# A third bank for the transposed scores of the fourth stage, its value products in the tail's bank, and a new order of all pieces

## What is computed

```python
x = x + _L0_attn_ref(_layernorm(x, axis=-1), L0_attn_w_q, L0_attn_w_k, L0_attn_w_v, L0_attn_w_o)
x = x + _L0_xattn_ref(16, 128, 256, L0_xattn_w, L0_xattn_u, _layernorm(x, axis=-1), ctx_2048)
x = x + _L0_ffn_ref(_layernorm(x, axis=-1), L0_ffn_w1, L0_ffn_w2, L0_ffn_w3)
x = x + _L1_attn_ref(_layernorm(x, axis=-1), L1_attn_Wq, L1_attn_Wk, L1_attn_Wv, L1_attn_Wo)
x = x + _L1_xattn_ref(_layernorm(x, axis=-1), ctx_2048, L1_xattn_Wq, L1_xattn_Wk, L1_xattn_Wv, L1_xattn_Wsk, L1_xattn_Wsv, L1_xattn_Wo)
x = x + _L1_ffn_ref(_layernorm(x, axis=-1), L1_ffn_W_base, L1_ffn_b_base, L1_ffn_A_s, L1_ffn_B_s, L1_ffn_A_r, L1_ffn_B_r, L1_ffn_W_router, L1_ffn_b_router)
```

```python
bias = jnp.concatenate([alibi, alibi], axis=-1)
delta = -rel
ssm_mask = (delta >= 0) & (delta < W_SSM)
att_mask = (delta >= 0) & (delta < W_ATT)
mask = jnp.concatenate([ssm_mask, att_mask], axis=-1)
scores = jnp.einsum('bhqd,bhkd->bhqk', q, k) / np.sqrt(D).astype(np.float32)
scores = scores + bias[None]
scores = jnp.where(mask[None, None], scores, -jnp.inf)
wei = jax.nn.softmax(scores, axis=-1)
return jnp.einsum('bhqk,bhkd->bhqd', wei, v)
```

## Time and profile before

| | us |
|---|---|
| median of 3 runs | 701.42 |
| lowest and highest | 701.37, 702.06 |
| span of the profiled execution | 699.8 |
| PE busy | 592.3 |
| DVE busy | 564.3 |
| ACT busy | 485.4 |
| POOL busy | 357.8 |

### The profile page before, as it was taken

The page is one execution under the profiler, slowest core; times in us unless marked ns, Lnnn a source line. Parts: engine busy times, 40 slices in busy tenths (PEclk is TensorE's granted clock), DMA queues, the critical chain, the costliest instruction groups (busy, mean ns, idle before and its releaser), DMA issues.

```text
span 699.8 us, 20088 instructions
## 1 busy us (share of the span) xinstructions
PE 592.3 (85%) x7268; PEld 351.6 (50%) x7268; DVE 564.3 (81%) x1487; ACT 485.4 (69%) x1197; POOL 357.8 (51%) x600
## 2 busy tenths in 40 slices
PE   0579789776688888999999978899999999989995
PEld 0256556454465667644444434454454445445653
DVE  5699988889989997879999767777777777777885
ACT  3689999887878756568888764577667677665531
POOL 3336766798999989766665312424323323312110
PEclk9999999988999999999999999999999999999998
DMA  7486984211110002545455534534444344320101
GB/s 268 106 171 148 243 118 92 65 58 50 45 39 31 24 1 51 76 77 77 78 78 84 98 54 82 99 74 71 78 86 71 66 89 76 53 49 19 39 32 37
DMA packets 162819, 55.16 MB, mean 79 GB/s; under 512 B 148961, under 2 KB 160545, under 8 KB 162465
## 3 DMA queue, kind: packets, MB, share of 16 engines
q1 hardware_dynamic: 160672, 53.75, 38.2%
q0 software_dynamic: 2048, 0.14, 0.2%
HBM read 16.89 MB, written 5.24 MB: 32 GB/s over the span
## 4 chain that ended last, share of the span: by engine, by line
PE 49%; POOL 14%; DVE 13%; issue 9%; ACT 6%; DMA 6%; SPq 3%; ACTq 0%; DVEq 0%; POOLq 0%
PE bank L1330 5%; DMA l1a_kT<-k_stack 3%; PE bank L1277 3%; PE bank L999 3%; PE bank L1302 3%; PE bank L1263 3%; POOL mix_hidden_parts L1493 2%; PE bank L1356 2%; PE bank L1284 2%; PE bank L987 2%; PE bank L1336 2%; PE bank L1306 2%; PE bank L1019 2%; PE bank L1859 2%; PE bank L960 2%
## 5 line engine op out<-in xcount | busy, mean ns | idle before, releaser
L1178 DVE TENSOR_REDUCE l1x_neg_max<-bank 128x2 f16<-128x448 f32 (+1 forms) x192 | 117.2, 639 | 35.4 <-PE bank L1284 34.1
L1232 ACT ACTIVATE l1x_probs<-bank 128x512 f32<-128x512 f32 x192 | 104.5, 596 | 51.3 <-PE bank L1316 28.9
L1134 POOL DMA_DIRECT2D l1x_qT<-l1x_neg_maxT x64 | 36.2, 577 | 136.4 <-ACT l1x_neg_maxT L1228 136.2
L886 DVE TENSOR_REDUCE l1a_neg_max<-bank 128x4 f16<-128x512 f32 x128 | 83.0, 680 | 15.2 <-PE bank L973 14.2
L933 ACT ACTIVATE l1a_probs<-bank 128x512 f32<-128x512 f32 x128 | 70.1, 598 | 20.4 <-PE bank L987 20.0
L1679 PE MATMUL bank<-mix_xT_parts,w_ternary 128*128 128x256 f16 x384 | 50.8, 284 | 10.1 <-DVE mix_hidden L1561 10.1
L1679 PEld LDWEIGHTS bank<-mix_xT_parts,w_ternary 128*128 128x128 f16 x384 | 37.6, 102 | 19.1 <-DVE mix_hidden L1561 7.9
L568 DVE TENSOR_REDUCE l_neg_max<-bank 128x4 f16<-128x512 f32 x64 | 41.9, 679 | 6.0 <-PE bank L697 5.8
L1493 POOL TENSOR_TENSOR mix_hidden_parts<-mix_hidden,mix_hidden_parts 128x256 f16<-128x256 f32 x48 | 37.8, 792 | 6.5 <-ACT mix_hidden_parts L1624 6.2
L640 ACT ACTIVATE l_probs<-bank 128x512 f32<-128x512 f32 x64 | 35.6, 621 | 1.4 <-PE bank L720 1.0
L1284 PE MATMUL bank<-l1x_kT,l1x_qT 64*64 64x224 f16 (+1 forms) x1024 | 36.2, 236 | 0.0
(11 more groups left out here) (266 smaller groups left out, 1741.4 us busy)
## 6 DMA issues: line engine op xcount, KB each, us to landing
ctx_projected<-mix_ctx_projected SPq DMA_DIRECT2D x16, 192.0 KB, 1.9
l1x_ctx_projected<-ctx_projected SPq DMA_DIRECT2D x16, 160.0 KB, 2.6
x_residual<-x_in SPq DMA_DIRECT2D x4, 512.0 KB, 4.7
mix_ctx_in<-ctx_in SPq DMA_DIRECT2D x16, 128.0 KB, 2.0
out_dram<-moe_out SPq DMA_DIRECT2D x16, 128.0 KB, 1.7
w_f<-w_in SPq DMA_DIRECT2D x2, 704.0 KB, 8.5
w_attn_f<-w_l_in SPq DMA_DIRECT2D x1, 1024.0 KB, 6.5
q_stack<-q_begin_in SPq DMA_DIRECT2D x1, 1024.0 KB, 5.2
```

Source lines behind the costliest of these rows:

```text
L886: dve.tensor_reduce(mm[:, 16 * j + 4 * s:16 * j + 4 * s + 4], b_s[c % 3][:].rearrange("p (r k) -> p r k", k=P), AX.X, ALU.max, negate=True ...
L1178: dve.tensor_reduce(mm[:, first:first + count], scores, AX.X, ALU.max, negate=True).then_inc(s_max, 1)
L1232: act.activation(prob[:, c, :], b_st[c % 2][:], ACT.Exp).then_inc(s_exp, 1)
```

## The change

The work of each instruction stays as it was, and none is added or taken away. Three things change.

**The fourth stage's banks.** ST rotates over banks 5, 6 and 7, so that step c needs one exp less than before; PV sums into bank 0, the tail's, and waits for the addition to x of the batch before (semaphore s_x), where it waited for ACT's copy of the last sum; T1 loses two waits.

**The order of the fourth stage and of all others.** One table PHASES gives each piece one virtual place relative to its batch. Its numbers are new for every stage, so the order differs on every engine.

**Setup and late loads.** Each step of the setup has its own virtual time in a table STEPS.

```diff
-    b_tail, b_proj, b_s, b_st, b_ot = banks[0], banks[1], banks[2:5], banks[5:7], banks[7]
+    b_tail, b_proj, b_s, b_st = banks[0], banks[1], banks[2:5], banks[5:8]
...
-                act.activation(prob[:, c, :], b_st[c % 2][:], ACT.Exp).then_inc(s_exp, 1)
+                act.activation(prob[:, c, :], b_st[c % 3][:], ACT.Exp).then_inc(s_exp, 1)
...
-                act.copy(ots[:, bp, :], b_ot[:]).then_inc(s_oe, 1)
+                act.copy(ots[:, bp, :], b_tail[:]).then_inc(s_oe, 1)
...
-                    take(pe, prev.left, 5, 6)
-                wait(pe, s_exp, 12 * b + 2 * c)
-                tiles = [(b_st[j][64 * u:64 * u + 64, :], slice(64 * j, 64 * j + 64), slice(64 * u, 64 * u + 64))
+                    take(pe, prev.left, 5, 6, 7)
+                wait(pe, s_exp, 12 * b + 2 * c - 1)
+                tiles = [(b_st[(2 * c + j) % 3][64 * u:64 * u + 64, :], slice(64 * j, 64 * j + 64), slice(64 * u, 64 * u + 64))
...
-                    take(pe, prev.left, 7)
+                    take(pe, prev.left, 0)
                 pe.wait_ge(s_exp, b * 12 + 6 * (c + 1))
-                wait(pe, s_oe, b)
+                wait(pe, s_x, b)
...
-                    pe.matmul(b_ot[32 * x:32 * x + 32, :], v_flat[:, b % 3, col:col + 32], prob[:, 6 * c + x, :],
+                    pe.matmul(b_tail[32 * x:32 * x + 32, :], v_flat[:, b % 3, col:col + 32], prob[:, 6 * c + x, :],
...
             elif piece == "T1":
                 pe.wait_ge(s_oe, b + 1)
-                wait(pe, s_t2, 2 * b)
-                if b == 0:
-                    take(pe, prev.left, 0)
-                wait(pe, s_x, b)
...
-            yield turn(LOADS[2] + LOADS[3] * k)
+            yield next(at)
             sp.dma_start(dst, src).then_inc(net.s_late, 16)
...
-                yield turn(SPREAD[1] + (3 * (m - 4) + z) * SPREAD[2])
+                yield next(at)
...
-    ("l1x", "pe"): order("""
-        S.4-2 F5 T1.0-4 S.5-2 ST.2-3 T4-4 F7 M-2 ST.3-3 T5-4 S.0-1 ST.4-3 PV.0-3 S.1-1 ST.5-3 S.2-1 ST.0-2 S.3-1
-        PV.1-3 ST.1-2"""),
...
+    ("l1x", "pe"): phases("""
+        F5@0.060 F7@0.261 S.0@1.559 S.1@1.678 S.2@1.742 S.3@1.805 S.4@2.033 S.5@2.136 M@2.352 ST.0@2.756 ST.1@3.044
+        ST.2@3.195 ST.3@3.338 ST.4@3.492 PV.0@3.607 ST.5@3.722 PV.1@3.853 T1@4.088 T4@4.328 T5@4.469"""),
```

More of the change, by code:

```diff
@@ new lines, in steps, with clock, pieces @@
+def steps(program, engine):
+    return iter(STEPS[program, engine])
+def clock(stage, n, turn):
+    start, fill, paces, drain = PACE[stage]
+    part = (n - 1) / len(paces)
+    run = sum(pace * min(max(turn - 1 - k * part, 0), part) for k, pace in enumerate(paces))
+    return start + fill * min(turn - 1, 0) + run + drain * max(turn - n, 0)
+def pieces(stage, engine, n):
+    placed = [(b + phase, k, name, arg, b) for k, (phase, name, arg) in enumerate(PHASES[stage, engine]) for b in range(n)]
+    for turn, _, name, arg, b in sorted(placed):
+        yield clock(stage, n, turn), name, arg, b, b % 2
@@ L233, in dve_program @@
     def dve_program(dve):
-        yield turn(SETUP[0])
+        at = steps("begin", "dve")
+        yield next(at)
         done = [0]
@@ L271, in dve_program @@
             abs_sum(m)
-        yield turn(SETUP[4])
+        yield next(at)
         dve.wait_ge(s_tot, 2)
@@ L287, in pe_program @@
     def pe_program(pe):
-        yield opening("l0")
+        at = steps("begin", "pe")
+        yield next(at)
         pe.wait_ge(s_dve, 4)
@@ L296, in act_program @@
     def act_program(act):
+        at = steps("begin", "act")
         for m in range(4):
-            yield turn(SETUP[1] + 0.04 * m)
+            yield next(at)
             src, dst = mats[m]
@@ L355, in clock @@
-def clock(stage, n, turn):
-    start, fill, paces, drain = PACE[stage]
-    part = (n - 1) / len(paces)
-    run = sum(pace * min(max(turn - 1 - k * part, 0), part) for k, pace in enumerate(paces))
-    return start + fill * min(turn - 1, 0) + run + drain * max(turn - n, 0)
-def pieces(stage, engine, n):
-    words = ORDERS[stage, engine]
-    shifts = [shift for _, _, shift in words]
-    for it in range(-max(shifts), n - min(shifts)):
-        for (name, arg, shift), part in zip(words, TIMES[stage, engine]):
-            b = it + shift
-            if 0 <= b < n:
-                yield clock(stage, n, it + part), name, arg, b, b % 2
@@ L374, in opening @@
-def opening(stage):
-    return clock(stage, 2, -max(shift for (name, _), words in ORDERS.items() if name == stage for _, _, shift in words))
 def merge(*programs):
@@ L397, in prepare_windows @@
 def prepare_windows(pool, net):
-    at = [clock("l0", NB, LOADS[4] + LOADS[5] * k) for k in range(9)]
-    yield at[0]
+    at = steps("windows", "pool")
+    yield next(at)
     pool.wait_ge(net.s_late, 16 * len(net.late_loads))
@@ L1428, in sp_program @@
     def sp_program(sp):
-        yield opening("mix")
+        yield from steps("mix", "sp")
         sp.wait_ge(net.s_ffn, 9)
@@ L1627, in pe_program @@
     def pe_program(pe):
-        yield opening("mix")
+        yield from steps("mix", "pe")
         pe.wait_ge(net.s_ffn, 9)
```

294 lines of the change are left out of this document (148 added, 146 removed).

## The result

The changed kernel takes 708.22 us (median of 4 runs, 707.19 to 709.73) against 701.39 us for the kernel before in the same comparison: a ratio of 1.0085, 95% interval 1.0062 to 1.0108. It is slower by about 6.8 us, and outside the stated range of 691 to 703. In the profiled executions the spans are 707.3 and 699.8, 7.5 us apart. Of the kernel before's 19 executions beside experiments 5 and 6, two ran slower throughout (733.73 and 774.26 us, at a mean granted clock of 0.841 and 0.756) and are left out of the ratios there, though not of the median 702.52.

A forecast was written before the change was run, and what follows sets the result against it. PE was taken as the bound, notably in the fourth stage. The extra bank's -3.8 us and the first stage's -0.2 gave -4.0; 699.8 - 4.0 + 1.6 = 697.4 us, range 691 to 703.

The forecast's parts named there:

- The loads in lumps (c): First stage, SP: late loads grouped behind later transposes lengthen landings, 2.2 us of stalls for 3.4; taken as +0.3 us.
- Rival D: First stage: each lump's full lengthening of landing reaches PE, +7.5 us, slower at 705.1; chance 0.07.
- rival E: Fourth stage: PE's short pauses over three rotating banks drop the granted clock to 1.2 GHz, about 716 us; chance 0.01.
- (a): First stage, DVE: two of three sums over FFN weights move forward to batch 1; -0.5 us, bounds -3.1 and +1.6.
- (b): First stage, POOL: nine weight roundings grouped behind copies and scales, no longer delaying the variance; -0.5 us, bounds -2.7 and +2.
- The extra bank: Fourth stage, PE: third ST bank removes ST.0's exp wait; gain 0.27 us a turn, 3.8 us over 14 turns.
- The value products in the tail's bank: Fourth stage: PV.0 now waits for the previous batch's last DVE addition; slack 0.47 us, so it costs nothing.
- Rival C: Fourth stage: PV.0 waits for a delayed addition, +0.52 us a turn, slower at 708.7; chance 0.05.
- The rows of maxima: Fourth stage: later M delays the DMAs ST.0 needs; 0.5 us median slack, up to 0.8 us a turn lost at worst.
- Rival B: The exp's 0.27 us return as a wait for maxima rows or T4's copy, first stage gives nothing: 701; chance 0.16.
- Second and third stages, ctx loads: Second and third stages: 0 each, bounds ±3 and ±2 us; first context loads behind all sixteen pairs: +0.5 us.
- rival A: Fourth stage also loses DVE's wait and the first stage gains 2 to 3 us: about 693; chance 0.18.

The follow-up runs named there:

- experiments 5 and 6: Changed kernel with late loads spread as before and M ahead of ST.3: 700.30 us; that plus PV.1 ahead of S.3: 703.51 us; kernel before 702.52.
- experiment 1: Changed kernel with its 17 late loads put back between the pairs of transposes: 699.76 us against 701.93 for the kernel before, ratio 0.9969.
- experiment 2: Kernel before with its late loads in the changed kernel's lumps: 709.23 us against 701.93, ratio 1.0087.
- experiment 4: Kernel before with the change of banks alone, every piece in its old order: 702.23 us against 701.93, ratio 1.0013.
- experiments 3 and 4: The first of these: changed kernel with M moved ahead of ST.3 on PE and ACT, 707.57 us against 701.93 for the kernel before; the other is experiment 4.
- experiment 10: Changed kernel with late loads spread, M ahead of ST.3 and the second stage's first two context loads issued earlier: 700.35 us against 702.25 for the kernel before.

## Why the prediction was wrong

**The loads in lumps (c)** is the step that failed. It was priced at +0.3 us and measured +8.5 (experiment 1), +7.3 (experiment 2). Seen along the traces: at the first stage's eleventh addition the changed kernel is 7.4 us behind (130.37 for 122.96), and at the end of the span 7.5. Rival D named it, at 705.1 and with a chance of 0.07; the step erred in not seeing it as the forecast. Three terms of the step were mis-sized, and the landing was not one of them: 3.2 + 5.1 = 8.3 us was forecast behind the second lump, and 7.1 was measured; behind the third 3.2 + 3.9 = 7.1, and 7.8 (from 99.98 to PE's start at 107.81).
- *The slack.* It was taken as 6.6 - 3.2 = 3.4 us from the start of the pair. But kT's issue stands behind qT's, and its landing counts from there. In the kernel after the pair's issue begins at 86.96 and PE wants it at 96.74 - 3.55 = 93.19, 6.2 us later, near the 6.6 assumed. An undisturbed pair needs 1.24 for qT's issue and 3.2 for kT's landing, so the slack was 1.8, not 3.4. Here 2.7 go to qT's issue and 7.1 to kT's landing: 9.8 - 6.2 = 3.6, the pause of 3.55. The kernel before could have told: by the step's own rule the landing of 6.7 us there is 6.7 - 3.2 - 3.4 = 0.1 us too late, and PE's wait for it was 1.48.
- *The issue.* Behind the second lump SP's issues took 2.64 and 5.04 us, for 1.23 to 1.41 from 116 us on. The loads and the pair behind them then started late, so that one lump delayed the next pair: on the chain, SP's instructions stand end to end from 89.64 to 99.93. This was named as a risk ("the transposes of one batch can push the next") and given 1.5 us (2.2 of stalls for 3.4 would be -1.2; +0.3 was taken). The stalls were 6.45 us, not 2.2.
- *The clock.* Behind the pauses of 3.55 and 2.90 us PE ran at a granted clock of 0.50 for over 3 and over 5 us, and its nine groups took 1.35 and 2.05 us more. A clock below 1.00 stood in the kernel before too, beyond 130 us (0.85 in 130:200), and this step had no term for it; rival E looked for it in the fourth stage alone. It cost 3.4 us.

**The sum of the first stage otherwise.** The terms (a) and (b) were -0.5 each; measured -1.0 and -0.5 alone, -2.7 in all, the last with the loads spread too. Most of it does not outlive the second stage, where DVE and POOL are full: in experiment 1 the last addition of the recurrence's output comes at 266.4 for 267.1, 0.7 us ahead. The third stage's last addition is 2.8 us ahead (438.3 for 441.1) and the fourth's 1.9 (677.4 for 679.3). No term of the sum had this, and what gains in the third stage was not taken apart.

**The extra bank.** The mechanism was right to the row: S.2 kept its 0.36 us, ST.0 followed without a wait, and S.3 waited for the third maximum, 2.05 us behind the first where 2.02 was forecast (506.13 - 504.11). The step failed in the value taken from it. The gain was read at the start of S.3's matmuls, as if they cost the same behind a pause. They cost 0.19 us more, and 0.27 became 0.04 a turn (experiment 4), 3.8 us became 14 x 0.04 = 0.6.

**The value products in the tail's bank.** Right: in 456:616 the value products wait for DVE's addition in no turn, neither in the kernel after nor in experiments 3 and 4. Rival C falls.

**The rows of maxima.** Forecast: 0.5 us of slack in the median, up to 0.8 a turn lost at the longest landing. Measured: no wait in 8 of 12 turns, and 1.0 us on average in each of 4, every third turn; the longest landing was 3.9 us, not 3.3. Rival B described this, but in the sum it had been set to nothing. It costs 0.21 us a turn (13.50 for 13.29) and turned the fourth stage's small gain into a loss.

**Second and third stages, ctx loads.** 0.5 us was set for the late context loads: experiment 10 shows none.

**A slip in rival A.** Its two sums give 693.9 and 695.4 us, not the "about 693" that stands behind them. Nothing hangs on it, since the time went the other way.

## What to carry to other kernels

Price a wait at the point where the engine is back in step, not where the waiting instruction starts: the next instructions may cost more behind a pause, and a wait that only changes its place gives back nearly nothing. A list of bulk loads between latency-bound transfers is to be spread over the turns; count the issuing engine's own time and the transfer's distance from the start of its own issue, and try the rule for the slack on a stall that the old trace already has. Where a table of times sets an order, look for the steps whose times fall below the one before: they go out as a lump.
